# A vision tower's routing stage: the shared network's contraction cut 128 + 64, and its list products one chunk later

## The reference, cut to what matters

```python
def _L0_ffn_ref(hidden_states, gate_weight, Wg, Wu, Wd, Ws_g, Ws_u, Ws_d):   # x: (8240, 192)
    scores = sigmoid(x @ gate_weight.T)                    # 16 experts
    topk_score, topk_ids = top_k(scores.T, 1030)           # each expert takes its 1030 best tokens
    xg = x[topk_ids]
    gate = silu(einsum('ecd,efd->ecf', xg, Wg)); up = einsum('ecd,efd->ecf', xg, Wu)
    out = einsum('ecf,edf->ecd', gate * up, Wd) * topk_score[..., None]
    y = zeros.at[topk_ids].add(out)
    shared = silu(x @ Ws_g.T) * (x @ Ws_u.T) @ Ws_d.T      # 192 -> 384 -> 192, on every token
    return y + shared
```

## Time and profile before

| | us |
|---|---|
| median of 3 runs | 4561.05 (4549.51 to 4570.84) |
| the profiled execution | 4569.56 |
| its span, first to last instruction | 4567.8 |
| retention, from the span's start | 138 to 459 |
| route, logits | 459 to 493 |
| route, bit loop | 493 to 633 |
| route, ranks and transposes | 633 to 656 |
| route, list loop and ids | 656 to 875 |

### The profile page before, as it was taken

How to read it: one execution, slowest core, us unless ns; L and a number is a source line. 1 busy time by engine, 2 the same in 40 slices (tenths; PEclk the granted TensorE clock), 3 DMA queues, 4 the chain that set the end, 5 groups by cost and what they waited for, 6 DMA issues and landing times. The chain is left out here.

```text
span 4567.8 us, 74772 instructions
## 1 busy us (share of the span) xinstructions
PE 4034.8 (88%) x23898; PEld 2458.2 (54%) x23898; DVE 2484.5 (54%) x4593; ACT 1438.0 (31%) x2890; POOL 1249.9 (27%) x1415
## 2 busy tenths in 40 slices
PE   8899878699999997665999999999959969899996
PEld 7788555466666665331333333333315646677774
DVE  1576468622222222876878787877814355444442
ACT  0122110011111111341677777777741111111111
POOL 0221010144444443553010001001012110077775
PEclk9999988899999998775999999999975589999998
DMA  6222111322222221345342224223225211267776
GB/s 217 60 67 54 32 38 28 99 61 60 60 60 60 60 60 28 118 132 107 49 62 44 44 48 61 44 44 51 39 62 158 76 37 46 66 163 172 174 172 154
DMA packets 335914, 361.61 MB, mean 79 GB/s; under 512 B 50364, under 2 KB 297107, under 8 KB 334095
## 3 DMA queue, kind: packets, MB, share of 16 engines
q1 hardware_dynamic: 252191, 274.75, 24.4%
q0 software_dynamic: 61312, 63.66, 8.9%
q10 hardware_dynamic: 22256, 20.93, 1.6%
HBM read 247.51 MB, written 117.00 MB: 80 GB/s over the span
## 5 line engine op out<-in xcount | busy, mean ns | idle before, releaser
L2033 DVE TENSOR_REDUCE at_mx<-psum 128x1 f32<-128x998 f32 (+1 forms) x768 | 884.5, 1189 | 247.2 <-PE psum L1858 246.8
L1988 ACT ACTIVATE at_p<-psum 128x512 f32<-128x512 f32 (+3 forms) x1536 | 851.2, 588 | 294.2 <-PE psum L1932 264.3
L1932 PE MATMUL psum<-at_q,at_k 99*128 99x512 bf16 (+3 forms) x1536 | 518.9, 380 | 21.5 <-issue 16.5
L1858 PE MATMUL psum<-at_k,at_q 96*128 96x512 bf16 (+3 forms) x1536 | 472.9, 390 | 69.4 <-POOL at_identb L1815 31.9
L1918 PE MATMUL psum<-at_p,at_v 128*32 128x486 f32 (+3 forms) x3072 | 405.1, 600 | 1.0 <-ACT at_p L1988 0.7
L1932 PEld LDWEIGHTS psum<-at_q,at_k 99*128 99x128 bf16 (+1 forms) x1536 | 155.0, 102 | 423.9 <-ACT at_p L1988 271.7
L1193 ACT ACTIVATE ex_silu<-psum 128x384 f32<-128x384 f32 (+1 forms) x288 | 131.5, 457 | 774.4 <-PE psum L1137 581.7
L1224 DVE TENSOR_TENSOR ex_hT<-ex_silu,psum 128x384 f32<-128x384 f32 (+1 forms) x288 | 147.5, 512 | 417.1 <-ACT ex_silu L1193 230.3
L1830 POOL DMA_DIRECT2D o_rows<-at_o x96 | 48.5, 505 | 1140.3 <-DVE at_mx L2033 967.0
L1159 PE MATMUL psum<-ex_wd,ex_hT 128*128 128x192 f32 (+1 forms) x1728 | 291.5, 327 | 0.0
L1858 PEld LDWEIGHTS psum<-at_k,at_q 96*128 96x128 bf16 (+1 forms) x1536 | 151.9, 105 | 230.6 <-DVE at_mx L2033 64.0
(11 more groups left out here) (361 smaller groups left out, 7030.7 us busy)
## 6 DMA issues: line engine op xcount, KB each, us to landing
mx_wd<-in_e_dT SPq DMA_DIRECT2D x72, 288.0 KB
qk_parts<-hd_parts SPq DMA_DIRECT2D x32, 579.4 KB, 3.8
at_k<-qk_parts SPq DMA_DIRECT2D x144, 128.8 KB, 5.0
at_q<-qk_parts SPq DMA_DIRECT2D x144, 124.8 KB, 4.6
tok_p<-in_x SPq DMA_DIRECT2D x12, 1176.0 KB
mx_wg<-in_e_gT SPq DMA_DIRECT2D x72, 192.0 KB
mx_wu<-in_e_uT SPq DMA_DIRECT2D x72, 192.0 KB
v_rows<-hd_v_out SPq DMA_DIRECT2D x8, 1536.0 KB
```

The lines of the kernel that those rows point to most:

```text
L1858: mm = pe.matmul(psum[0:ctx_rows[t], 3 + 2 * ((PRO + n) % 2) + k, 0:w], Q[v][0:R6, j * 1024 + 128 * t:j * 1024 + 128 * t + ctx_rows[t]], K ...
L1932: pe.matmul(psum[0:n, i % RING, 0:w], K[u][:, j, 128 * t:128 * t + n], Q[u][:, j * 1024 + at:j * 1024 + at + w], start=True, stop=True).th ...
L1988: act.activation(P[0:n, c % 2, j, 0:w], psum[0:n, i % RING, 0:w], ACT.Exp).then_inc(exp_ready, 1)
L2033: dve.tensor_reduce(mx[0:ctx_rows[t], j * CT + t:j * CT + t + 1], pair(n)[0:ctx_rows[t], 0:CTX], AX_X, ALU.max).then_inc(s_free, 1)
```

## The change

- `x1T` becomes 128 partitions x 2. Its first plane holds features 0 to 127; the second holds features 128 to 191 on partitions 0 to 63. `turn_x1` transposes the columns 0 to 127 and 64 to 191, and ScalarE copies all 128 rows of the one and rows 64 to 127 of the other.
- `gate` and `gpad` follow (L846 becomes two copies per image). The shared network's weights become `wg` and `wu` (128 features) and `wr` (64 of gate below, 64 of up above). Eight constant transfers become eleven.
- The matmuls of `shared_up` are now gate and up on 128 features, and a remainder of two matmuls on 64 partitions each: gate's on partitions 0 to 63, up's on 64 to 127. The remainder comes last in slices 0 and 2 and first in slice 1.
- The remainder's moving data must lie on both halves of the partitions: a new buffer `xr`, which GpSimd fills twice from `x1T` for every tile (`pair_up`), each time behind a 16 x 1 addition. GpSimd waits before it until all of the tile before has gone through `shared_up`. TensorE waits for both copies before slice 0.
- GpSimd's order: `pair_up` for the ten rounds of the bit loop, then the 20 transfers of the scores, then `pair_up` for the ten chunks of the list loop.
- The list products of a chunk are issued between `shared_up` and `shared_down` of the next chunk's tile; the first tile's up and down stand ahead of the loop and the last chunk's list products behind it.

```diff
-    return buffers(ctx, nc, "rt", gate=(DP, DC, E0), ..., wg=(DP, DC, FS0), wu=(DP, DC, FS0), wd=(128, FS0 // 128, D))
+    return buffers(ctx, nc, "rt", gate=(128, 2, E0), ..., wg=(128, FS0), wu=(128, FS0), wr=(128, FS0), wd=(128, FS0 // 128, D))
...
-ROUTE_CONSTS = 16 * 8
+ROUTE_CONSTS = 16 * 11
...
-                            last = pe.transpose(psum[0:DP, 2 * g + m, b * T:(b + 1) * T],
-                                                x_out[:, g * HB + b, m * DP:(m + 1) * DP], ident[0:T, 0:T])
+                            last = pe.transpose(psum[:, 2 * g + m, b * T:(b + 1) * T],
+                                                x_out[:, g * HB + b, m * (D - 128):m * (D - 128) + 128], ident[0:T, 0:T])
...
-                        act.activation(x1T[:, m, g * HB:(g + 1) * HB, bass.ds(c * T, T)],
-                                       bank(2 * g + m, DP, W4).rearrange("p (b t) -> p b t", b=HB),
+                        act.activation(x1T[0:(128, D - 128)[m], m, g * HB:(g + 1) * HB, bass.ds(c * T, T)],
+                                       psum[(0, 64)[m]:128, 2 * g + m, 0:W4].rearrange("p (b t) -> p b t", b=HB),
...
+        xr = sb("sh_xr", [128, W4])
+        zero32 = sb("sh_zero32", [128, 1])
+        carried = sb("sh_carried", [128, 2])
...
+            pool.memset(zero32[:], 0.0).then_inc(zeroed, 1)
+            pool.wait_ge(zeroed, 4)
+            def pair_up(j):
+                pool.wait_ge(u_full, j * FC)
+                for half in range(2):
+                    pool.tensor_tensor(carried[0:16, half:half + 1], zero32[0:16], zero32[0:16], ALU.add)
+                    pool.tensor_copy(xr[64 * half:64 * half + 64], x_flat[0:64, 1, bass.ds(j * W4, W4)]).then_inc(xr_ready, 1)
+                    pool.wait_ge(xr_ready, j * 2 + (half + 1))
+            with pool.Fori(0, LOOPS) as j:
+                pair_up(j)
             pool.wait_ge(turned_out, 9)
             for c in range(NC):
...
+            with pool.Fori(LOOPS, 2 * LOOPS) as j:
+                pair_up(j)
...
             for f in slices:
-                for w, n, full in ((wg, 0, g_full), (wu, 1, u_full)):
-                    for k in range(DC):
-                        last = pe.matmul(psum[:, 2 * (f % 2) + n, 0:W4], w[:, k, f * 128:(f + 1) * 128],
-                                         x_flat[:, k, bass.ds(j * W4, W4)], start=(k == 0), stop=(k == 1))
-                    last.then_inc(full, 1)
+                if f == 0:
+                    pe.wait_ge(xr_ready, j * 2 + 2)
+                def most(first):
+                    g = pe.matmul(gate, wg[:, cols], toks, start=first, stop=not first)
+                    u = pe.matmul(lift, wu[:, cols], toks, start=first, stop=not first)
+                    return g, u
+                def remainder(first):
+                    g = pe.matmul(gate, wr[0:64, cols], xr[0:64], start=first, stop=not first)
+                    u = pe.matmul(lift, wr[64:128, cols], xr[64:128], start=first, stop=not first)
+                    return g, u
+                if f % 2 == 0:
+                    most(True)
+                    g, u = remainder(False)
+                else:
+                    remainder(True)
+                    g, u = most(False)
+                g.then_inc(g_full, 1)
+                u.then_inc(u_full, 1)
...
-            with pe.Fori(0, NC // 2) as i:
+            shared_up(pe, LOOPS)
+            shared_down(pe, LOOPS)
+            with pe.Fori(0, NC // 2 - 1) as i:
                 for half in range(2):
                     c = i * 2 + half
-                    shared_up(pe, c + LOOPS)
-                    shared_down(pe, c + LOOPS)
-                    pe.wait_ge(hot_ready, c + 1)
...
-                    last.then_inc(hot_used, 1)
+                    shared_up(pe, c + LOOPS + 1)
+                    list_rows(c, half)
+                    shared_down(pe, c + LOOPS + 1)
+            shared_up(pe, NC - 1 + LOOPS)
+            list_rows(NC - 2, 0)
+            shared_down(pe, NC - 1 + LOOPS)
+            list_rows(NC - 1, 1)
...
             for b in range(B):
-                last = dve.tensor_copy(gpad[:, :, b, b * E0:(b + 1) * E0], gate[:])
+                dve.tensor_copy(gpad[:, 0, b, b * E0:(b + 1) * E0], gate[:, 0, :])
+                last = dve.tensor_copy(gpad[0:64, 1, b, b * E0:(b + 1) * E0], gate[0:64, 1, :])
```

More of the change, by code:

```diff
@@ L239, in route_consts @@
 def route_consts(ctx, nc):
-    return buffers(ctx, nc, "rt", gate=(DP, DC, E0), same=(128, 128), before=(128, 128), consts32=(T, ROUTE_COLS), row=(T, 1),
-                   wg=(DP, DC, FS0), wu=(DP, DC, FS0), wd=(128, FS0 // 128, D))
+    return buffers(ctx, nc, "rt", gate=(128, 2, E0), same=(128, 128), before=(128, 128), consts32=(T, ROUTE_COLS), row=(T, 1),
+                   wg=(128, FS0), wu=(128, FS0), wr=(128, FS0), wd=(128, FS0 // 128, D))
 def load_route_consts(queue, inp, c, arrived):
-    for dst, src in ((c["gate"][:], inp["gateT"].rearrange("(c p) e -> p c e", c=DC)),
+    for dst, src in ((c["gate"][:, 0, :], inp["gateT"][0:128]), (c["gate"][0:64, 1, :], inp["gateT"][128:D]),
                      (c["same"][:], inp["rt_same"]), (c["before"][:], inp["rt_before"]),
                      (c["consts32"][:], inp["rt_iota"]), (c["row"][:], inp["rt_row"]),
-                     (c["wg"][:], inp["sh_gT"].rearrange("(c p) f -> p c f", c=DC)),
-                     (c["wu"][:], inp["sh_uT"].rearrange("(c p) f -> p c f", c=DC)),
+                     (c["wg"][:], inp["sh_gT"][0:128]), (c["wr"][0:64], inp["sh_gT"][128:D]),
+                     (c["wu"][:], inp["sh_uT"][0:128]), (c["wr"][64:128], inp["sh_uT"][128:D]),
                      (c["wd"][:], inp["sh_dT"].rearrange("(c p) d -> p c d", c=FS0 // 128))):
         queue.dma_start(dst, src).then_inc(arrived, 16)
-ROUTE_CONSTS = 16 * 8
+ROUTE_CONSTS = 16 * 11
 def phase_retention(nc, psum, inp, h0, h1, xg, x1T, ident, ident_in, ret, consts_in, route, route_in):
@@ L620, in phase_route @@
         gate, same, before, consts32, row = (consts[n] for n in ("gate", "same", "before", "consts32", "row"))
-        wg, wu, wd = (consts[n] for n in ("wg", "wu", "wd"))
-        gpad = sb("rt_gpad", [DP, DC, B, 128])
+        wg, wu, wr, wd = (consts[n] for n in ("wg", "wu", "wr", "wd"))
+        gpad = sb("rt_gpad", [128, 2, B, 128])
+        xr = sb("sh_xr", [128, W4])
+        zero32 = sb("sh_zero32", [128, 1])
+        carried = sb("sh_carried", [128, 2])
         iota_lo = sb("rt_iota_lo", [T, LB], BF16)
@@ L670, in phase_route @@
         d_full, y_ready = sem("sh_d_full"), sem("sh_y_ready")
-        h_loaded, y_stored = sem("sh_h_loaded"), sem("sh_y_stored")
+        h_loaded, y_stored, xr_ready = sem("sh_h_loaded"), sem("sh_y_stored"), sem("sh_xr_ready")
         x_flat = x1T.rearrange("p c b n -> p c (b n)")
@@ L706, in _ @@
                         .then_inc(scores_out, 16)
+            with pool.Fori(LOOPS, 2 * LOOPS) as j:
+                pair_up(j)
             pool.wait_ge(scores_out, 32 * NC)
         def shared_up(pe, j, slices=range(FC)):
+            toks = x_flat[:, 0, bass.ds(j * W4, W4)]
             for f in slices:
[L712 to L717 removed]
+                if f == 0:
+                    pe.wait_ge(xr_ready, j * 2 + 2)
+                pe.wait_ge(hT_ready, j * FC + max(f - 1, 0))
+                gate, lift = psum[:, 2 * (f % 2), 0:W4], psum[:, 2 * (f % 2) + 1, 0:W4]
+                cols = slice(f * 128, (f + 1) * 128)
+                def most(first):
[14 more added lines that the diff above has]
+                u.then_inc(u_full, 1)
         def shared_down(pe, j, halves=range(2)):
@@ L736, in _ @@
                 for b in range(B):
-                    for k in range(DC):
-                        last = pe.matmul(psum[:, s, 0:n], gpad[:, k, b, :], x1T[:, k, b, s * W4:s * W4 + n],
+                    for k, r in enumerate((128, D - 128)):
+                        last = pe.matmul(psum[:, s, 0:n], gpad[0:r, k, b, :], x1T[0:r, k, b, s * W4:s * W4 + n],
                                          start=(b == 0 and k == 0), stop=(b == B - 1 and k == 1))
@@ L775, in _, with list_rows @@
             pe.wait_ge(turned_out, 9)
-            with pe.Fori(0, NC // 2) as i:
+            def list_rows(c, half):
+                pe.wait_ge(hot_ready, c + 1)
+                for b in range(B):
+                    for e in range(E0):
+                        q, g = e % 2, e // 2
+                        last = pe.matmul(psum[LB * q:LB * q + 2 * HB2, 6, g * LB:(g + 1) * LB],
+                                         hot_hi[:, half, b * E0 + e, :], hot_lo[:, half, b * E0 + e, :],
+                                         start=False, stop=False, skip_group_check=True)
+                last.then_inc(hot_used, 1)
+            shared_up(pe, LOOPS)
+            shared_down(pe, LOOPS)
+            with pe.Fori(0, NC // 2 - 1) as i:
                 for half in range(2):
                     c = i * 2 + half
-                    shared_up(pe, c + LOOPS)
```

(7 more changed lines are left out.)

2 lines of the change are left out of this document (1 added, 1 removed).

## The result

The changed kernel takes 4593.11 us (4584.75 to 4603.51, 5 runs) against 4561.05: 1.0068 of before, interval 1.0047 to 1.0090, so 21 to 41 us slower. The forecast was 4548, and 4593.11 lies above its range. The profiled execution of the changed kernel took 4585.24 us, its span is 4583.4.

The account below looks back on a forecast made before the run. VectorE was taken to bound the list loop with a hole per chunk, TensorE the bit loop by little. 0.3 + 0.9 - 2.8 - 36.2 + 17.0 + 8 = -12.8 us, from median 4561.05: 4548; range 4526 to 4568.

Parts of the forecast that it names:

- the logits, put at nothing: Route's logits and scores: no term forecast for their passes.
- the cost of a change of row form, 0.19 us: Read from the experts' stage: going to the 64-row form or back costs 0.19 us each way.
- The clock rival: List loop: TensorE stays at half clock behind its idle, +81 us on the forecast, 4629; chance 0.05.
- The waits that go (-36.2): List loop: VectorE's 37.4 us of waits for TensorE go but for the first chunk's 1.17, -36.2 us.
- The first wait (+17.0): List loop's start: the first tile's xr stands behind 20 score transfers in GpSimd's queue, +17.0 us.
- The port (+8): List loop: GpSimd's additions and copies slow VectorE at the shared port, 0.9 us a chunk, nine chunks, +8 us.
- The rate of 0.72: Retention: scalings L550 lost 2.04 us for 2.8 us of GpSimd beside them, applied to the list loop.
- The bit loop (-2.8): Bit loop: shorter slices bring the third product earlier, 0.28 us per round, -2.8 us for ten.
- Retention (+0.3): Retention: transposes load 128 columns for 96, +0.3 us in all.
- The head (+0.9): Route's head: eight more copies into gpad and one small memset before the first logits, +0.9 us.
- The first `pair_up`, put beside the logits and at nothing: Route's head: GpSimd's first filling of xr runs beside the logits and costs nothing.
- forecast at -13.1 us: Route: head +0.9, logits none, bit loop with ranks and transposes -2.8, list loop and ids -11.2; sum -13.1 us.

Follow-up runs that it names:

- e5: Changed kernel with 24 unused 128-row matmuls ahead of the logits to warm TensorE; one execution, logits 36.7 us, route 417.4 us.
- e1: Changed kernel with each bank's logits passes grouped by row form, 6 form changes instead of 48; 0.9977 of the kernel before.
- e2: Changed kernel with the logits' second pass on all 128 rows, the lower 64 against zero weights, order unchanged; 0.9973 of the kernel before.
- e4: Kernel before with the list products one chunk later and nothing else, no cut at 128, no copies; 0.9933 of the kernel before.
- e3: Changed kernel with GpSimd filling xr for the eleventh tile before the 20 score transfers; 1.0027 of the kernel before.
- e9: Changed kernel with logits grouped by row form, eleventh tile's xr before the score transfers, remainder first in all slices; 0.9930 of the kernel before.
- e11: Changed kernel with logits grouped by two images, 24 changes of row form instead of 48; one execution, route 403.7 us.

## Why the prediction was wrong

**The step that failed: the logits, put at nothing without a reason; they took 39.4 us more.** The prediction priced the copies into `gpad` ahead of them and went on; it held the cost of a change of row form, 0.19 us, in its hand and applied it to the shared network's four changes per tile only. The logits' loop changes form on every pass, 48 times with the step to the bit loop, because its operands now have 128 and 64 rows. At the price read from the earlier trace rows that was 9 us on the critical chain, which would have brought the forecast to 4557; e5 confirms the price. The larger part, some 30 us, no row of before showed: that this rhythm keeps a cold clock from rising (e1, e2, e5).

**The clock rival named the right resource in the wrong place.** It looked for half clock in the list loop. There the changed kernel runs at 0.99 from 715 to 820, and over the whole list loop and ids at 0.91 where the kernel before had 0.88; the stretch:

```profile
715.00:820.00 105.00, 81.62 (x938) 51.83 (x934) 103.41 (x79) 10.29 (x20) 43.62 (x24) 0.99 0.13 34
```

**The waits that go (-36.2): right.** e4 shows -38.1 for the list loop and ids by themselves.

**The first wait (+17.0): right.** 18.65 against 1.17 before, +17.5, and e3 takes 14.6 us of it away by the order in GpSimd's queue alone.

**The port (+8): too large.** The rate of 0.72 came from a scaling instruction, L550, and was carried to instructions with two inputs. Groups of the changed kernel's list loop show who pays:

```profile
L710 POOL TENSOR_TENSOR sh_carried<-sh_zero 16x1 f32<-16x1 f32 x20 | 36.5, 1823 | 90.6 <-PE psum L743 89.7
L711 POOL COPY sh_xr<-x1T 64x412 f32 x20 | 29.4, 1470 | 0.4
...
L983 DVE TENSOR_TENSOR rt_wide<-rt_hit,rt_tile 103x2176 bf16<-103x2176 bf16 x9 | 23.7, 2631 | 0.3
```

A chunk loses 0.2 us on VectorE, 1.8 in all (L983 has 2631 ns where L937 had 2427), and GpSimd's four instructions take 6.6 us where they would take 1.4. A chunk is 17.34 us, e4's without copies 17.1 to 17.2. The Trainium skill ("SBUF — State Buffer", SBUF: two separate sides) has the pair of ports held by whichever instruction starts first, the other standing still. The trace agrees on GpSimd's side, whose addition lasts as long as the piece beside it (2.15 against 2.29 us). On VectorE's side the list loop does not bear it out in full: L974 and L979 have 2285 and 2419 ns with the copies, where L928 and L933 had 2284 and 2418, and only L983, behind the piece beside which GpSimd's copy stood, is longer, by 0.20 us, less than the copy's own 0.52. Timeline of the changed kernel:

```profile
775.68 2.42 DVE L979 TENSOR_TENSOR rt_hit<-rt_hiT,rt_iota_hi 103x2176 bf16<-103x2176 bf16 x1
775.85 2.63 POOL L711 COPY sh_xr<-x1T 64x412 f32 x1
778.13 2.63 DVE L983 TENSOR_TENSOR rt_wide<-rt_hit,rt_tile 103x2176 bf16<-103x2176 bf16 x1
```

Elsewhere VectorE does stand still. The prediction said that the trace of before has no VectorE instruction with two inputs beside a GpSimd one; it has one, in another stage:

```profile
3416.56 5.59 DVE L2320 TENSOR_TENSOR pr_on<-pr_op,pr_recip 128x1030 f32<-128x1030 f32 x2 [11.60 <-DMA pr_hin<-y_rows]
3416.67 4.39 POOL L2207 TENSOR_TENSOR pr_hb<-pr_hin,pr_bias 128x1536 f32<-128x1536 f32 x1 [16.50 <-issue]
```

The second of these two L2320 took 4.44 us, where the median of the sixteen is 1.21, and ended 1.09 us after GpSimd's addition did. So which engine loses depends on the case; why VectorE loses so little in the list loop stays open.

**The bit loop (-2.8): -0.7.** A round takes 13.90 us for 13.97. The mechanism was right, but slice 2's chain was 0.3 us longer than worked out: its first pass comes 5.92 after the start, not 5.8, its last pair 2.01 behind that, not 1.9, and silu to product is 0.60 us, not 0.54, which leaves 9.08. The first round also starts at low clock after the logits: this part of route takes 164.0 us, and 162.1 in e1, where the clock is high.

**Retention (+0.3): nothing. The head (+0.9): +1.4.** The first `pair_up`, put beside the logits and at nothing, ran beside the copies into `gpad`, and two of those, 0.16 us alone, took 0.63 and 0.50:

```profile
459.01 0.63 DVE L892 COPY rt_gpad<-rt_gate 64x16 f32<-64x16 f32 x1
459.10 0.52 POOL L711 COPY sh_xr<-x1T 64x412 f32 x1
```

Without the logits route was forecast at -13.1 us and measured at -17.1, from one trace of each kernel. That these lie only 4 us apart is in part luck: the list loop came out 8.4 us better than forecast, 6 of them the port, and the bit loop with ranks and transposes 3.9 us worse. The direction was lost by the one loop that was read as unchanged.

## What to carry to other kernels

When an operand is cut into parts of different height, list every loop that reads it and count how often each goes from one row form to the other; group the passes by form, which cost nothing here, where they add into the same bank. A shorter pass earns only what it moves at the instruction that waits for it: order the passes so that the result with the longer way behind it ends first. A helper's small copies belong ahead of a block of transfers in the same queue, not behind.

What is worth keeping of this change is the new order of the list loop alone (e4, 0.9933) or all of it repaired (e9, 0.9930); the two can't be told apart, and e4 is the simpler.

## What was not expected of the hardware

- A rhythm of two records on 128 and two on 64 rows, TensorE never idle, ran 69 us at half clock after a cold start (in two traces, the changed kernel's and e3's), and 37 us at full clock after a warm one (e5). With 24 changes instead of 48 the clock rose after 8.9 us (e11, one trace), with 6 after 2.8 to 5.8 us (five traces).
- A change of row form cost 0.20 us at full clock (e5) and 0.29 at half.
- A 16 x 1 addition on GpSimd took 0.18 us alone and 1.82 in the mean beside VectorE's stream of one-hot instructions, of which L983 alone was longer, by 0.20 us. Two single copies of VectorE, of 0.16 us, took 0.63 and 0.50 beside GpSimd's copy.
